# First increment of q kept scaled, its identity product in stage 3 replaced by a GpSimd sum

## The reference, cut to what matters

```
def _derivative(q, p, drive, coupling, bias):
    i_couple = jnp.tanh(q) @ coupling.T
    dq = q - q ** 3 / 3.0 - p + drive + i_couple + bias
    dp = EPSILON * (q + ALPHA - BETA * p)
    return (dq, dp)

dq1, dp1 = _derivative(q, p, drive, coupling, bias)
dq2, dp2 = _derivative(q + 0.5 * DT * dq1, p + 0.5 * DT * dp1, drive, coupling, bias)
dq3, dp3 = _derivative(q + 0.5 * DT * dq2, p + 0.5 * DT * dp2, drive, coupling, bias)
dq4, dp4 = _derivative(q + DT * dq3, p + DT * dp3, drive, coupling, bias)
q_next = q + DT / 6.0 * (dq1 + 2 * dq2 + 2 * dq3 + dq4)
```

## Time and profile before

| | us |
|---|---|
| median of 3 runs (595.29 to 595.6) | 595.32 |
| the profiled execution: its own time | 597.59 |
| the profiled execution: its span | 595.8 |
| PE busy | 573.1 (96%) |
| VectorE (DVE) busy | 482.9 (81%) |
| ScalarE (ACT) busy | 399.0 (67%) |
| GpSimd (POOL) busy | 253.3 (43%) |

### The profile page before, as it was taken

One profiled execution on the slowest core, in us unless ns is written; L12 is line 12 of the kernel. 1 busy time (PEld: TensorE's weight loads), 2 busy tenths in 40 slices (PEclk: granted clock), 3 DMA queues, 4 the chain that ended last, 5 costly groups with the idle time before them and its releaser, 6 DMA issues.

```text
span 595.8 us, 16005 instructions
## 1 busy us (share of the span) xinstructions
PE 573.1 (96%) x6012; PEld 520.6 (87%) x6012; DVE 482.9 (81%) x1330; ACT 399.0 (67%) x980; POOL 253.3 (43%) x400
## 2 busy tenths in 40 slices
PE   9999999999999999999979999999999999999996
PEld 8899999999999988887868888888888888888884
DVE  3777777767677758777689999999999999999996
ACT  3545454454454376685456888888888888888884
POOL 0423323323232145421245555555555555556550
PEclk9999999999999999999899999999999999999999
DMA  8400000000000001500000000000000000000000
GB/s 270 180 2 2 1 1 2 1 1 2 2 1 1 19 3 37 142 21 2 2 1 2 11 19 10 19 19 10 20 19 10 19 19 10 19 20 10 19 27 30
DMA packets 13165, 15.01 MB, mean 25 GB/s; under 512 B 1760, under 2 KB 11296, under 8 KB 13088
## 3 DMA queue, kind: packets, MB, share of 16 engines
q1 hardware_dynamic: 13088, 13.98, 7.3%
HBM read 9.78 MB, written 4.19 MB: 23 GB/s over the span
## 4 chain that ended last, share of the span: by engine, by line
PE 67%; DVE 18%; ACT 6%; issue 5%; DMA 1%; POOL 1%; SPq 1%; DVEq 0%; ACTq 0%
PE PS L492 21%; PE PS L325 17%; PE PS L348 13%; PE PS L551 4%; DVE q_s L1130 4%; PE PS L573 4%; PE PS L466 3%; DVE h_s L1116 2%; PE PS L410 2%; DVE h_s L1103 2%; DVE h_s L1109 2%; DVE PS L1079 2%; ACT k_s L800 2%; PE PS L419 1%; ACT big L730 1%
## 5 line engine op out<-in xcount | busy, mean ns | idle before, releaser
L492 PE MATMUL PS<-k_s,h_s 128*128 128x128 f32 x1024 | 140.1, 280 | 8.9 <-ACT k_s L800 8.3
L492 PEld LDWEIGHTS PS<-k_s,h_s 128*128 128x128 f32 x1024 | 126.1, 191 | 19.7 <-issue 14.5
L325 PE MATMUL PS<-part 128*128 128x256 f32 x900 | 115.6, 286 | 0.0
L325 PEld LDWEIGHTS PS<-part 128*128 128x128 f32 x900 | 109.8, 191 | 0.0
L800 ACT ACTIVATE k_s<-h_s 128x128 f32<-128x128 f32 x256 | 65.2, 301 | 47.3 <-DVE h_s L1109 37.0
L348 PE MATMUL PS<-big,wrk 128*128 128x128 f32 x744 | 88.4, 275 | 2.2 <-DVE big L958 2.2
L348 PEld LDWEIGHTS PS<-big,wrk 128*128 128x128 f32 x744 | 85.8, 192 | 2.8 <-DVE big L958 2.8
L1267 POOL COPY h_s<-big 128x256 f32<-128x256 f32 x32 | 21.4, 670 | 129.0 <-DVE big L958 129.0
L492 PE MATMUL PS<-h_s 128*128 128x128 f32 x384 | 61.6, 283 | 0.4 <-DVE PS L1098 0.4
L689 ACT ACTIVATE big<-big 128x256 f32<-128x256 f32 x32 | 13.3, 416 | 63.9 <-DVE big L940 63.9
L492 PEld LDWEIGHTS PS<-h_s 128*128 128x128 f32 x384 | 50.4, 191 | 3.1 <-DVE PS L1098 0.6
(11 more groups left out here) (188 smaller groups left out, 1198.8 us busy)
## 6 DMA issues: line engine op xcount, KB each, us to landing
out<-q_s SPq DMA_DIRECT2D x32, 128.0 KB, 1.7
x_s<-in_xT SPq DMA_DIRECT2D x14, 256.0 KB, 6.2
k_s<-in_wgT SPq DMA_DIRECT2D x4, 208.0 KB, 2.5
k_s<-in_wuT SPq DMA_DIRECT2D x4, 208.0 KB, 2.7
k_s<-in_wih SPq DMA_DIRECT2D x3, 256.0 KB, 4.5
wrk<-in_whh SPq DMA_DIRECT2D x3, 256.0 KB, 5.1
h_s<-in_wdT SPq DMA_DIRECT2D x3, 256.0 KB, 3.5
x_s<-in_xT SPq DMA_DIRECT2D x4, 128.0 KB, 3.6
```

The source lines that it names most:

```text
L325: r = pe.matmul(p, y, x, start=i == 0, stop=i == len(passes) - 1)
L492: return pe.matmul(cm(stage_bank(slot), m), w, x, start=False, stop=True, skip_group_check=True)
```

## The change

The factor of the identity product, 2 - 2 kap, moves into the number that is stored: qs[1] is now kept multiplied by it (`held`), through the factor with which `nexts` of stage 1 reads the bank (`of_ps`). The cubic term of stages 1 and 2, the scales of tanh and square of stage 2 and two steps of the p update (t3, t4) get factors that take this into account. These are constants in instructions that stood there before. With qs[1] stored so, the stage-3 term is a plain sum: GpSimd adds qs[1] to dq in place, in a new instruction behind dq, and `seed_4` waits for it (s_dq now counts two per step). The identity product of stage 3, its scaled identity id_z3 and the copy that made it are gone; the wait in front of the oscillator is for 3 instead of 4 of these copies. Tiles behind id_z3 in the work area move by 128 columns or more, as their names' tensors in the rows below show (WZ goes from q_s to h_s).

```diff
--- before.py
+++ after.py
@@ -57,7 +57,9 @@
     cube = (c / 3, c / 3, 2 * c / 3, c / 9)
     own = (3 + 3 / c, 3.0, 3.0, 3 + 3 / c)
     lam = 3 / c4
-    of_ps = (3.0, 3.0, -6.0)
+    held = (1.0, 1.0, 2 - 2 * kap, 1.0)
+    gain = (1.0, held[2], 1.0, 1.0)
+    of_ps = (3.0, 3.0 * held[2], -6.0)
     q_next = lambda t, s, m: 6 * t + 2 * s + m + 1
 
     with ExitStack() as ctx:
@@ -152,7 +154,7 @@
             return areas[0][:, at:at + n]
 
         coupU = halves(take(512))
-        id_q1, id_s2, id_z3 = (take(128) for _ in range(3))
+        id_q1, id_s2 = (take(128) for _ in range(2))
         qn = [take(256) for _ in range(2)]
         pn = [take(256) for _ in range(2)]
         qs = [take(256) for _ in range(3)]
@@ -510,7 +512,7 @@
 
             pe.wait_ge(s_add, 13)
             keep_warm(3, 9)
-            pe.wait_ge(s_cp, 4)
+            pe.wait_ge(s_cp, 3)
             for t in range(T):
 
                 if t >= 1:
@@ -560,7 +562,6 @@
                 coupled(4 * t + 2)
                 if t == 0:
                     keep_warm(7, 3)
-                linear(4 * t + 3, id_z3, qs[1])
                 if t >= 1:
                     i = t - 1
                     if i:
@@ -798,10 +799,10 @@
                     else:
                         ac.wait_ge(s_next, q_next(slot // 4, s - 1, m))
                     ac.activation(cm(th[slot % 2], m), cm(src, m), ACT.Tanh,
-                                  scale=(-1 if s == 3 else 1) / lam).then_inc(s_th, 1)
+                                  scale=(-1 if s == 3 else 1) / (lam * held[s])).then_inc(s_th, 1)
                 if slot == 0:
                     ac.wait_ge(s_F, 16)
-                ac.activation(sqP, src, ACT.Square, scale=math.sqrt(cube[s]) / lam).then_inc(s_sq, 1)
+                ac.activation(sqP, src, ACT.Square, scale=math.sqrt(cube[s] * gain[s] / held[s]) / (lam * held[s])).then_inc(s_sq, 1)
 
             for t in range(T):
 
@@ -1092,7 +1093,7 @@
                                         ALU.add).then_inc(s_seed, 1)
 
             def seed_4(t):
-                ve.wait_ge(s_dq, t + 1)
+                ve.wait_ge(s_dq, 2 * t + 2)
                 ve.wait_ge(s_WZ, t + 1)
                 ve.wait_ge(s_next, q_next(t, 1, 1))
                 ve.scalar_tensor_tensor(stage_bank(3), dq, 1 / 3, WZ, ALU.mult, ALU.add).then_inc(s_seed, 1)
@@ -1100,7 +1101,7 @@
             def cubic(slot, src):
                 s = slot % 4
                 ve.wait_ge(s_sq, slot + 1)
-                ve.scalar_tensor_tensor(w_, sqP, cube[s] * own[s], src, ALU.subtract, ALU.mult).then_inc(s_w, 1)
+                ve.scalar_tensor_tensor(w_, sqP, cube[s] * own[s] * gain[s] / held[s], src, ALU.subtract, ALU.mult).then_inc(s_w, 1)
 
             def nexts(slot, dst):
                 ve.wait_ge(s_w, slot + 1)
@@ -1186,14 +1187,14 @@
                                             ALU.mult).then_inc(s_thh, 1)
                 if t < T - 1:
                     ve.wait_ge(s_t2, t + 1)
-                    ve.scalar_tensor_tensor(t3, t2, horner[2], qs[1], ALU.mult, ALU.add).then_inc(s_t3, 1)
+                    ve.scalar_tensor_tensor(t3, t2, horner[2] * held[2], qs[1], ALU.mult, ALU.add).then_inc(s_t3, 1)
                 if t >= 2:
                     ve.wait_ge(s_thh, i + 1)
                     ve.reciprocal(h_at(i, 4), h_at(i, 1)).then_inc(s_s2, 1)
                 if t < T - 1:
                     ve.wait_ge(s_t3, t + 1)
                     ve.wait_ge(s_next, q_next(t, 2, 1))
-                    ve.scalar_tensor_tensor(t4, t3, horner[3], qs[2], ALU.mult, ALU.subtract).then_inc(s_t4, 1)
+                    ve.scalar_tensor_tensor(t4, t3, horner[3] / held[2], qs[2], ALU.mult, ALU.subtract).then_inc(s_t4, 1)
                 cubic(4 * t + 3, qs[2])
                 last_next(t)
                 if t < T - 1:
@@ -1300,7 +1301,7 @@
                     po_.wait_ge(s_Vp, 16)
                     po_.wait_ge(s_P, 8)
                     po_.tensor_scalar(coupU, coup, U, 0.0, ALU.mult, ALU.add).then_inc(s_cp, 1)
-                    for dst, f in ((id_q1, (1 - kap) / 3), (id_s2, -kap / 3), (id_z3, (2 - 2 * kap) / 3)):
+                    for dst, f in ((id_q1, (1 - kap) / 3), (id_s2, -kap / 3)):
                         po_.tensor_scalar(dst, ident[:, :], f, 0.0, ALU.mult, ALU.add).then_inc(s_cp, 1)
 
 
@@ -1329,6 +1330,9 @@
                 po_.tensor_tensor(two(WZ), two(uz), I_at(t), ALU.add).then_inc(s_WZ, 1)
                 po_.wait_ge(s_next, q_next(t, 0, 1))
                 po_.tensor_tensor(dq, qs[0], q, ALU.subtract).then_inc(s_dq, 1)
+                po_.wait_ge(s_dq, 2 * t + 1)
+                po_.wait_ge(s_next, q_next(t, 1, 1))
+                po_.tensor_tensor(dq, dq, qs[1], ALU.add).then_inc(s_dq, 1)
                 if t >= 4:
                     i = t - 4
 
```

## The result

The changed kernel takes 615.94 us (median of 4 runs, 614.41 to 618.76) against 595.31 us before (4 runs). The ratio is 1.035, with a 95% interval of 1.0316 to 1.0384: 3.5% slower. The forecast was 614.8 us, with 611.5 to 620.5 as the range. What the title calls the first increment is qs[1], the result of stage 1; the next tanh reads it directly (line 800), so it is a scaled q and not an increment. For the timing that makes no difference.

The account below looks back on a forecast made before the run. The prediction took VectorE's queue to bound stages 0 to 2 and TensorE stage 3. Adding 29 x (0.70 - 0.08) = 18.0, 0.8 and 0.7 us to 595.32 gave 614.8 us, range 611.5 to 620.5.

Parts of the forecast that it names:

- The late seed: Stage 2 on VectorE: seed_4 waits for GpSimd's sum and starts 0.70 us late per step, bounds 0.69 to 0.81.
- Nothing covers it on VectorE: Stage 2: VectorE works in order, nexts follows seed_4 by 0.77 us, so the full 0.70 us goes onto the chain.
- The gain of 0.08 us in stage 3: Stage 3 on TensorE: without the identity product it lasts 2.06 instead of 2.14 us; bounds of the gain 0 and 0.17.
- three stages on VectorE's queue and one on TensorE: One oscillator step: stages 0, 1 and 2 are bound by VectorE's queue, stage 3 by TensorE, with 0.46 us VectorE idle.
- 18.0 + 0.7 = 18.7: Oscillator: 18.0 us lost over steps 2 to 30, 29 x (0.70 - 0.08), plus 0.7 in step 1.
- nothing in step 31: Last step: GpSimd doesn't wait for t2, the sum ends at about 577.76, seed_4 stands at 577.78 already: 0 added.
- Step 0 adds its 0.8: Step 0: seed_4 already waits for dq, so the sum's 0.08 + 0.73 is all added, 0.81 us.
- the 19.5 worked out: Whole kernel: total loss of 18.0 + 0.8 + 0.7 = 19.5 us, 3.3% slower.
- hidden: Rival: GpSimd ends the sum before VectorE reaches seed_4, only the gain of 2.5 us stays, 592.8 us; chance 0.04.
- slowed beside VectorE: Rival: the GpSimd sum takes 0.38 us more per step beside VectorE's work, 12 us more, 627 us; chance 0.05.
- TensorE's gap before stage 3's product: Stage 3: TensorE would sit idle for some 0.8 us before coupled in every step.
- the clock rival: Rival: TensorE's clock falls after its idle time, stage 3's product takes 1.80 instead of 1.13 us, 636 us; chance 0.02.

Follow-up runs that it names:

- e2: Kernel before, identity product kept, with GpSimd's sum of dq and qs[1] written to an unread spare tile and seed_4 waiting for it: 620.84 us, ratio 1.0401.
- e3: Changed kernel with seed_4 moved behind the stage-2 result in VectorE's order: 602.49 us, ratio 1.012.
- e6: Changed kernel with uz ahead of u3 on GpSimd and seed_4 between the cubic term and the result of stage 2: 596.09 us, ratio 1.0002.
- e9: Changed kernel with uz made by ScalarE and seed_4 between the cubic term and the result of stage 2: 590.9 us, ratio 0.9929.
- e1: Changed kernel without GpSimd's new sum, the qs[1] term left out of seed_4, which waits for dq alone: 593.28 us, ratio 0.9954.
- e4: Changed kernel with GpSimd's wait for t2 moved from in front of uz to in front of dq: 601.37 us, ratio 1.0103.
- e5: Changed kernel with uz moved to the start of GpSimd's step, ahead of u3: 602.5 us, ratio 1.0095.

## Why the prediction was right

**The late seed, 0.70 us.** Measured 0.71 (stage 2 from 2.10 to 2.81), from the parts named: a gap of 0.09 behind dq, 0.73 of the sum and 0.03 to VectorE's start, less the 0.15 us by which dq used to be ahead. e2 shows it alone.

**Nothing covers it on VectorE.** From the seed to the stage-2 result there are still 0.79 us (0.77 before). e3, e6 and e9 show the other side: with the seed behind work that VectorE does meanwhile, stage 2 lasts 2.00 us with the sum in place.

**The gain of 0.08 us in stage 3.** Measured 0.09; e1 shows it alone. The prediction's picture behind it, three stages on VectorE's queue and one on TensorE, leaves something out. Of the kernel before, the shares of the chain by engine over the whole span, then two pieces of that chain in step 16, stage 1's product and stage 3's:

```profile
PE 67%; DVE 18%; ACT 6%; issue 5%; DMA 1%; POOL 1%; SPq 1%; DVEq 0%; ACTq 0%
...
440.71 1.58 PE PS L492 x12
...
445.56 0.91 PE PS L492 x8
```

Between these two the chain stays on TensorE without a break. So TensorE had no idle time from stage 1's product to stage 3's either, and the identity product stood on the chain; but e1 shows that the next longest way, over VectorE and the tanh, was only 0.09 us per step shorter, and that is all that taking 0.71 us of product out could give.

**The sum.** From the first to the last `last_next` the changed kernel takes 298.33 us (298.96 to 597.29) and the one before 279.63 (301.14 to 580.77): 18.7 us more. The working had 18.0 + 0.7 = 18.7 for these 31 steps, with nothing in step 31. In that last step the seed starts with no idle time in front, though the sum ends just before it, which its rows show:

```profile
593.62 0.73 POOL L1335 TENSOR_TENSOR q_s<-q_s,h_s 128x256 f32<-128x256 f32 x1 [0.37 <-DVE h_s L1110]
...
594.38 0.43 DVE L1099 SCALAR_TENSOR_TENSOR PS<-q_s,h_s 128x256 f32<-128x256 f32 x1
```

Step 0 adds its 0.8. The medians differ by 20.6 us, 1.1 more than the 19.5 worked out. That rest isn't in the profiled steps; the profiled run itself, at 614.41, lies within 0.4 us of the forecast, and the other three, at a lower mean clock, lie 1 to 4 us above the forecast. On the chip of e1 to e4 the kernel before took 594.9 us (median of 11) at a mean clock of 0.999 or 1.00 and 598.6 (median of 5) below that, so the clock can account for the rest; that it does was not tested.

**The rivals.** The sum was not hidden. It was not slowed beside VectorE: 0.724 to 0.731 us in all steps. TensorE's gap before stage 3's product came, at 1.00 us where some 0.8 were forecast, and in the profiled execution no fall of the clock with it. Whether launches at a lower clock became more frequent is open: e1, without the product, had 10 of 12 below 0.999, the kernel before 5 of 16 on the same chip, but e6, also without it, only 2 of 12. Where the prediction's argument against the clock rival claimed too much is told in the last section.

## What to carry to other kernels

An engine with half its time idle can still have a deadline with 0.15 us to spare: before giving it work, look for what waits for its next result, and where that waiter stands in its own queue. Taking 0.71 us of matmuls per step off a TensorE that looks 96% busy, and that had most of the chain, gave 0.09 us per step, because another way, over VectorE and the tanh, was almost as long: before taking work off the chain, look how far behind it the next longest way is. When a late input can't be made earlier, move its reader: with the seed in a place where VectorE waits for TensorE anyway, and uz on ScalarE, the same sum makes the kernel faster than either (e9).

## What the runs showed of the hardware

VectorE operations with two SBUF inputs and GpSimd's instructions take turns in these traces, and the one that begins second pays. VectorE operations that began with 0.2 us or more of a GpSimd instruction still to run took longer: t4 0.83 instead of 0.42 us (e3), t2 0.54 instead of 0.40 (e4), `seed_1` 0.52 instead of 0.42 (e5), `seed_2` 0.62 instead of 0.43 (e6), the last back at 0.42 when uz left GpSimd (e9). In the lines shown each of the four ends 0.27 to 0.28 us behind the end of the GpSimd instruction, whatever the overlap. The other way round, e4's WZ began beside t2 and ended 0.59 us behind it, and before the change dq of step 1 ended 0.58 us behind VectorE's line 1030, which has a single input, in bf16. The cubic term, one of whose inputs lies in PSUM, took 0.40 to 0.43 us from step 2 on in all twelve traces, with GpSimd beside it or without. The Trainium skill, GPSIMD Engine Reference, section 1, names VectorE instructions with two SBUF inputs as a case of contention, and the traces agree. To keep GpSimd away from t2 is what the wait in front of uz was good for: e4 took it away from there and paid 0.14 us in stage 1.

The granted clock of TensorE falls in some executions and not in others, behind the same idle time. Between steps 1 and 2 eleven of the twelve profiles have a gap of 1.58 to 1.61 us in front of the feed-forward block's second product (line 600 in e1). In e1's the stretch around it was granted 0.69, and the first `coupled` of the next step took 1.79 us instead of 1.06; in the other ten the clock stayed at 1.00, in the kernel before and in the changed kernel, which had idled 1.57 us shortly before as well. e1, that product, the next step's first `coupled`, and the stretch; then the changed kernel, the same:

```profile
309.90 1.54 PE L600 MATMUL PS<-h_s,q_s 128*128 128x416 bf16 x4 [1.61 <-ACT q_s L859]
...
311.67 1.79 PE L494 MATMUL PS<-k_s,h_s 128*128 128x128 f32 x8
...
308.40:312.00 3.60, 2.10 (x8) 1.42 (x9) 1.69 (x5) 2.02 (x5) 2.04 (x4) 0.69 0.00 0
```

```profile
310.92 0.86 PE L600 MATMUL PS<-h_s,q_s 128*128 128x416 bf16 x4 [1.61 <-ACT q_s L859]
...
311.84 1.06 PE L494 MATMUL PS<-k_s,h_s 128*128 128x128 f32 x8
...
309.41:313.01 3.60, 2.09 (x17) 1.85 (x18) 2.35 (x7) 2.02 (x5) 2.07 (x4) 1.00 0.00 0
```

One execution in which a gap did no harm, as the prediction used it, is no proof against the clock.
